# Last row and tail of a two-layer graph kernel: weight tiles in row slots, a written-out order, a two-pass last norm

## The reference

```python
def layer0(h, adj, W1, W2, b):          # h: 4096x128, adj: 4096x4096, K = 16
    node = h @ W1
    hw = einsum('nc,kcf->nkf', h, W2)
    x = einsum('nk,nkf->nf', node, hw)
    return relu(adj @ x + node @ b)
def layer1(z, dist, W, B):
    msg = z @ W + B
    weights = where(dist < 1, exp(-(1 / dist - 1) ** 2 / (2 * 0.5 ** 2)), 0)
    return weights @ msg
x = layernorm(x + layer0(x, adj, ...))
x = layernorm(x + layer1(x, adj, ...))
```

## Time and profile before

| | |
|---|---|
| median of three runs | 572.2 us |
| the profiled execution, its own time | 571.83 us |
| its span | 570.0 us |
| TensorE busy | 557.1 us (98%) |
| ScalarE busy | 506.7 us (89%) |
| VectorE busy | 478.5 us (84%) |
| granted TensorE clock, mean | 0.998 |
| DMA queue 1, share of 16 engines | 66.5% |

### The profile page before, as it was taken

The page is one execution under the profiler, slowest core; times in us unless marked ns, Lnnn a source line. Parts: engine busy times, 40 slices in busy tenths (PEclk is TensorE's granted clock), DMA queues, the critical chain, the costliest instruction groups (busy, mean ns, idle before and its releaser), DMA issues.

```text
span 570.0 us, 5196 instructions
## 1 busy us (share of the span) xinstructions
PE 557.1 (98%) x1794; PEld 328.4 (58%) x1794; DVE 478.5 (84%) x524; ACT 506.7 (89%) x458; POOL 82.8 (15%) x74
## 2 busy tenths in 40 slices
PE   9999999999999999999999999999999999979896
PEld 7888888555555645565556555655565556534344
DVE  6777777998959997998899979997998899779553
ACT  5788878799999999999998999899989998678984
POOL 2889999100000000000000000000000000000000
PEclk9999999999999999999999999999999999999999
DMA  5991000599988878888889878887888774462012
GB/s 170 411 419 44 20 1 0 197 385 424 385 314 322 298 293 295 314 317 305 302 301 341 303 287 315 308 326 282 324 325 324 280 298 148 147 221 75 0 55 92
DMA packets 23129, 142.04 MB, mean 249 GB/s; under 512 B 2720, under 2 KB 3264, under 8 KB 6720
## 3 DMA queue, kind: packets, MB, share of 16 engines
q1 hardware_dynamic: 22960, 141.46, 66.5%
q10 hardware_dynamic: 144, 0.26, 0.2%
HBM read 139.62 MB, written 2.10 MB: 249 GB/s over the span
## 4 chain that ended last, share of the span: by engine, by line
PE 68%; ACT 17%; DVE 9%; issue 4%; DMA 1%; SPq 0%; DVEq 0%; ACTq 0%
PE l_ps L452 20%; PE acc_ps L414 9%; PE kept_ps L452 6%; ACT wt_pair L573 5%; PE hw_ps L377 5%; PE hw_ps L383 5%; PE hw_ps L380 5%; ACT wt_pair L578 5%; DVE wt_pair L748 4%; PE acc_ps L405 4%; PE acc_ps L404 4%; PE acc_ps L403 4%; ACT wt_pair L583 3%; DVE wt_pair L742 3%; ACT wt_pair L593 2%
## 5 line engine op out<-in xcount | busy, mean ns | idle before, releaser
L452 PE MATMUL l_ps<-wt_pair,msg 128*128 128x512 f32 x376 | 168.9, 592 | 2.2 <-DVE sumT L793 2.2
L742 DVE SCALAR_TENSOR_TENSOR wt_pair<-wt_pair 128x2048 f32<-128x2048 f32 x64 | 146.0, 2284 | 7.4 <-DMA wt_pair<-adjT_dram 7.3
L573 ACT ACTIVATE wt_pair<-wt_pair 128x4096 f32<-128x4096 f32 (+1 forms) x37 | 116.5, 3147 | 3.4 <-DVE wt_pair L742 3.4
L452 PEld LDWEIGHTS l_ps<-wt_pair,msg 128*128 128x128 f32 x376 | 70.7, 190 | 84.4 <-issue 80.4
L578 ACT ACTIVATE wt_pair<-wt_pair 128x4096 f32<-128x4096 f32 (+1 forms) x37 | 116.9, 3159 | 1.2
L414 PE MATMUL acc_ps<-row_in,x 128*128 128x512 f32 x216 | 96.8, 592 | 0.0
L560 ACT ACTIVATE prods<-hw_ps,node 128x128 f32<-128x128 f32 x256 | 73.0, 373 | 17.3 <-PE hw_ps L383 15.7
L590 ACT ACTIVATE wt_pair<-wt_pair 128x4096 f32<-128x4096 f32 (+1 forms) x19 | 62.0, 3262 | 27.4 <-DVE wt_pair L748 27.4
L735 DVE TENSOR_TENSOR row_lo<-row_in,adj_hi 128x2048 fp32r<-128x2048 f32 x37 | 84.8, 2292 | 1.3
L748 DVE SCALAR_TENSOR_TENSOR wt_pair<-wt_pair 128x4096 f32<-128x4096 f32 (+1 forms) x19 | 75.4, 3969 | 9.7 <-ACT wt_pair L578 9.7
L702 DVE SCALAR_TENSOR_TENSOR part_acc<-hw_ps,node,part_acc 128x128 f32<-128x128 f32 x224 | 60.7, 344 | 19.2 <-PE hw_ps L383 19.2
(11 more groups left out here) (84 smaller groups left out, 491.9 us busy)
## 6 DMA issues: line engine op xcount, KB each, us to landing
row_in<-adjT_dram SPq DMA_DIRECT2D x64, 1024.0 KB, 4.8
wt_pair<-adjT_dram SPq DMA_DIRECT2D x64, 1024.0 KB, 4.8
x_in<-xT_dram SPq DMA_DIRECT2D x8, 256.0 KB, 4.0
x_row<-xT_dram SPq DMA_DIRECT2D x8, 256.0 KB, 5.1
outT_dram<-sumT SPq DMA_DIRECT2D x7, 256.0 KB, 2.0
W_in<-W_dram SPq DMA_DIRECT2D x3, 256.0 KB, 5.2
W_in<-W_dram ACTq DMA_DIRECT2D x1, 256.0 KB, 3.8
outT_dram<-sumT SPq DMA_DIRECT2D x2, 128.0 KB, 1.8
```

The source lines that it names most:

```text
L452: mm = pe.matmul(out, msg[:, c % 2, k, :], wt[t % WT_RING][:, k, :], start=(first and k == 0), stop=(last and k == CH - 1))
L573: act.activation(w, w, ACT.Ln, bias=TINY).then_inc(ln_made, 1)
L742: dve.scalar_tensor_tensor(out=w, in0=w, scalar=1.0, in1=w, op0=ALU.is_lt, op1=ALU.mult).then_inc(mask_made, 1)
```

## The change

Four things are changed:

1. Weight tiles 60 to 63 are loaded into the first four *row* slots (`IN_ROWS = 60`), as soon as row tiles 60 to 63, which lie there, are done; they have their own semaphores, and they are masked singly and go through ln and inverse in pairs like the others.
2. From step 56 on (`TAIL = 56`) the order on ScalarE and VectorE is written out: the whole last row and the tail. ScalarE's log and exp of a norm are separate steps now (`log_variance`, `inverse_root`), with other work between them.
3. From tile 54 on (`BY_TILE`) the square and the last exp are done by tile, 128 x 2048, where they were done by pair. From tile 50 on (`THIRD_FROM`) the shared banks are three, with `acc_ps[:, 0]` as the third. The banks of the last norm are dealt anew.
4. In units 3 to 6 of the last norm (`TWO_PASS`) centre and variance run on rounded operands: VectorE casts the operand and subtracts for the remainder (into `adj_hi`, which is free by then), and TensorE runs one matmul on each. The two matrices are rounded once, at step 32.

```diff
 SPLIT = (1, 3, 4, 5, 7)
 SPLIT_FIRST = ((3, 5, 7), (1, 3, 5, 7))
+SPLIT_LAST = (1, 3, 4, 5, 7)
 SPLIT_LEAD = 2
 
 
 FIRST_STEPS = (0, 3, 5, 7, 10, 12)
 FIRST_PAIR = len(FIRST_STEPS)
-DVE_FROM = 54
-LAST_PAIR = 60
-
-TAIL = 66
+
+BY_TILE = 54
+
+IN_ROWS = 60
+
+THIRD_FROM = 50
+
+TAIL = 56
+
+TWO_PASS = (3, 6)
 
 ...
 
 
     def in_pair(m):
-        return FIRST_PAIR <= m < LAST_PAIR
+        return m >= FIRST_PAIR
 
 
     groups = [m for m in range(TILES) if not in_pair(m) or m % 2 == 0]
     group_of = [len([m for m in groups if m <= t]) - 1 for t in range(TILES)]
 
     def is_split(i):
+        if i // NB == NB - 1:
+            return i % NB in SPLIT_LAST
         return i % NB in (SPLIT_FIRST[i // NB] if i < 2 * NB else SPLIT)
 
     def on_dve(m):
         if in_pair(m):
-            return (m - FIRST_PAIR) % 4 >= 2 or m >= DVE_FROM
-        return m >= LAST_PAIR
+            return (m - FIRST_PAIR) % 4 >= 2 or m >= BY_TILE
+        return False
 
     split_tiles = [i for i in range(TILES) if is_split(i)]
-    dve_groups = [m for m in groups if on_dve(m)]
+
+    parts = [m for m in groups if m < BY_TILE] + list(range(BY_TILE, TILES))
+    part_of = [len([m for m in parts if m <= t]) - 1 for t in range(TILES)]
+    dve_parts = [m for m in parts if on_dve(m)]
     act_groups = [m for m in groups if not on_dve(m)]
 
 ...
+    def in_two_pass(u):
+        return TWO_PASS[0] <= u <= TWO_PASS[1]
+
+
+    shared = [t for t in range(TILES) if t % NB >= KEPT]
+    bank_of, before = {}, {}
+    for n, t in enumerate(shared):
+        late = len([s for s in shared if THIRD_FROM <= s < t])
+        bank_of[t] = t % L1_BANKS if t < THIRD_FROM else (L1_BANKS + late) % (L1_BANKS + 1)
+        same = [s for s in shared[:n] if bank_of[s] == bank_of[t]]
+        before[t] = same[-1] if same else None
 
     def row_added_step(r):
         return NB * (r + 1) + (3 if r < NB - 1 else 2)
 ...
+            rows = sb("rows", [P, ROW_RING, CH, BW], F32, whole)
+            row_in = [rows[:, s, :, :] for s in range(ROW_RING)]
 ...
+        wt = [wt_pair[t % WT_RING // 2][:, t % 2, :, :] if t < IN_ROWS else row_in[t - IN_ROWS] for t in range(TILES)]
 ...
+        y2_hi = [adj_hi[0][:, s, :] for s in range(2)]
+        y2_lo = [adj_hi[0][:, 2 + s, :] for s in range(2)]
+        sq2_hi = [adj_hi[1][:, s, :] for s in range(2)]
+        sq2_lo = [adj_hi[1][:, 2 + s, :] for s in range(2)]
 ...
+        shared_ps = [l1_ps[:, 0, :], l1_ps[:, 1, :], acc_ps[:, 0, :]]
+        yc2_banks = [acc_ps[:, 1, :], yc_ps[:, :], kept_ps[:, 0, :]]
+        yc2_ps = [yc2_banks[u % 3][:, 0:width(u)] for u in range(UNITS)]
+
+        var2_ps = [var_ps[:, 0:width(u)] for u in range(UNITS - 1)] + [shared_ps[bank_of[LAST - 2]][:, 0:HALF_BW]]
+
+        last_ps = [shared_ps[bank_of[LAST]][:, 0:HALF_BW], kept_ps[:, 1, 0:HALF_BW]]
 ...
+            def load_last_wt(t):
+
+                sp.wait_ge(row_tile_done, t + 1)
+                sp.dma_start(wt[t], adjT[t % NB, t // NB]).then_inc(last_wt_in[t - IN_ROWS], 16)
 ...
+                if IN_ROWS <= i < TILES:
+                    load_last_wt(i)
                 t = i - COL_LAG
-                if t >= 0 and t + WT_RING < TILES:
+                if t >= 0 and t + WT_RING < IN_ROWS:
                     load_wt(t + WT_RING)
 ...
                 if j >= KEPT:
-
-                    at_least(pe, sum_added, added_to(t - L1_BANKS - (KEPT if j < KEPT + L1_BANKS else 0)))
-                    out, first, last = l1_ps[:, j % L1_BANKS, :], True, True
+                    if before[t] is not None:
+
+                        pe.wait_ge(sum_added, added_to(before[t]))
+                    elif t >= THIRD_FROM:
+
+                        pe.wait_ge(y_made, NB - 1)
+                    out, first, last = shared_ps[bank_of[t]], True, True
                 else:
                     out, first, last = kept_ps[:, j, :], c == 0, c == NB - 1
-                pe.wait_ge(wts_made, group_of[t] + 1)
 ...
-                pe.wait_ge(sum_added, added_to(LAST - L1_BANKS if half == 0 else TILES - NB))
-                pe.wait_ge(wts_made, group_of[LAST] + 1)
+                pe.wait_ge(sum_added, added_to(before[LAST] if half == 0 else TILES - NB + 1))
+                pe.wait_ge(wts_made, part_of[LAST] + 1)
 ...
             def centre2(u):
+                at_least(pe, out_made, u - 2)
+                if in_two_pass(u):
+                    pe.wait_ge(rounded_w_made, 2)
+                    pe.wait_ge(y2_lo_made, u - TWO_PASS[0] + 1)
+                    pe.matmul(yc2_ps[u], centre_r[:, :], y2_hi[u % 2], start=True, stop=False)
+                    pe.matmul(yc2_ps[u], centre_r[:, :], y2_lo[u % 2], start=False, stop=True).then_inc(yc2_made, 1)
+                    return
                 pe.wait_ge(sum_added, added_to(TILES - NB - 1) + u + 1)
-                if u < NB - 2:
-                    at_least(pe, out_made, u - 2)
-                if u == UNITS - 1:
-
-                    pe.wait_ge(out_made, 4)
                 pe.matmul(yc2_ps[u], centre_w[:, :], sumT[:, unit(u)], start=True, stop=True).then_inc(yc2_made, 1)
 
             def variance2(u):
+                if u < UNITS - 1:
+                    at_least(pe, ln_var2_made, u)
+                else:
+
+                    pe.wait_ge(sum_added, added_to(LAST - 2))
+                if in_two_pass(u):
+                    pe.wait_ge(sq2_lo_made, u - TWO_PASS[0] + 1)
+                    pe.matmul(var2_ps[u], mean_r[:, :], sq2_hi[u % 2], start=True, stop=False)
+                    pe.matmul(var2_ps[u], mean_r[:, :], sq2_lo[u % 2], start=False, stop=True).then_inc(var2_made, 1)
+                    return
                 pe.wait_ge(sq2_made, u + 1)
-                if u == UNITS - 2:
-
-                    pe.wait_ge(out_made, 5)
-                else:
-                    at_least(pe, ln_var2_made, min(u, NB - 1))
                 pe.matmul(var2_ps[u], mean_w[:, :], sq[:, u % 2, 0:width(u)], start=True,
                           stop=True).then_inc(var2_made, 1)
 ...
             def take_exp(m):
-                w = weights(m)
+                w = part(m)
                 if on_dve(m):
 
-                    act.wait_ge(dve_square_made, dve_groups.index(m) + 1)
+                    act.wait_ge(dve_square_made, dve_parts.index(m) + 1)
                     act.activation(w, w, ACT.Exp, bias=-2.0, scale=-2.0).then_inc(wts_made, 1)
                 else:
 ...
-                at_least(act, var2_made, u - 1)
+                if in_two_pass(u - 2):
+
+                    act.wait_ge(sq2_lo_made, u - 2 - TWO_PASS[0] + 1)
+                else:
+                    at_least(act, var2_made, u - 1)
                 act.activation(sq[:, u % 2, 0:width(u)], yc2_ps[u], ACT.Square).then_inc(sq2_made, 1)
+
+            def log_variance2(u):
+                act.wait_ge(var2_made, u + 1)
+                at_least(act, out_made, u - 1)
+                act.activation(rstd[:, u % 2, 0:width(u)], var2_ps[u], ACT.Ln, bias=EPS).then_inc(ln_var2_made, 1)
 
             def inverse_root2(u):
 ...
+            take_exp(46)
+            square(6)
 ...
+            take_exp(54)
+            take_inverse(56)
+            take_exp(55)
+            square(7)
+            take_ln(58)
+            log_variance(7)
+            take_exp(56)
+            inverse_root(7)
+            take_inverse(58)
 ...
+            def round_unit(u):
+                dve.wait_ge(sum_added, added_to(TILES - NB - 1) + u + 1)
+                if u < TWO_PASS[0] + 2:
+                    dve.wait_ge(row_tile_done, TILES)
+                else:
+                    dve.wait_ge(yc2_made, u - 1)
+                dve.tensor_copy(y2_hi[u % 2], sumT[:, unit(u)]).then_inc(y2_hi_made, 1)
+
+            def remainder_of_unit(u):
+                dve.wait_ge(y2_hi_made, u - TWO_PASS[0] + 1)
+                dve.tensor_tensor(y2_lo[u % 2], sumT[:, unit(u)], y2_hi[u % 2], ALU.subtract).then_inc(y2_lo_made, 1)
+
+            def round_square2(u):
+                dve.wait_ge(sq2_made, u + 1)
+                if u < TWO_PASS[0] + 2:
+                    dve.wait_ge(row_tile_done, TILES)
+                else:
+                    dve.wait_ge(var2_made, u - 1)
+                dve.tensor_copy(sq2_hi[u % 2], sq[:, u % 2, :]).then_inc(sq2_hi_made, 1)
+
+            def remainder_of_square2(u):
+                dve.wait_ge(sq2_hi_made, u - TWO_PASS[0] + 1)
+                dve.tensor_tensor(sq2_lo[u % 2], sq[:, u % 2, :], sq2_hi[u % 2], ALU.subtract).then_inc(sq2_lo_made, 1)
 ...
+                if i == TILES // 2:
+                    dve.wait_ge(mean_w_filled, 1)
+                    dve.tensor_copy(mean_r[:, :], mean_w[:, :]).then_inc(rounded_w_made, 1)
+                    dve.wait_ge(centre_w_filled, 2)
+                    dve.tensor_copy(centre_r[:, :], centre_w[:, :]).then_inc(rounded_w_made, 1)
 ...
+            residual(7)
+            mask(60)
+            mask(59)
+            add_part(50)
 ...
+            round_unit(5)
```

(3 more changed lines are left out.)

216 lines of the change are left out of this document (144 added, 72 removed).

## The result

| | before | changed |
|---|---|---|
| median | 572.0 us (571.64 to 574.16, 4 runs) | 563.59 us (562.16 to 565.01, 4 runs) |
| profiled execution, its own time | 571.83 us | 562.98 us |
| its span | 570.0 us | 561.2 us |

The ratio is 0.9837 with an interval of 0.9805 to 0.9868: 1.6% faster. The forecast was 562.9 us. The two profiled executions are 8.85 us apart, against 9.35 in the sum.

A forecast was written before the change was run, and what follows sets the result against it. TensorE bounds up to row tile 63, waits between engines matter only behind it. Savings of 5.75 + 3.2 + 0.4 = 9.35 us off 571.8 give 562.5, with 0.4 us offset a median of 562.9 us; range 561.5 to 567.0.

The forecast's parts named there:

- What bounds the kernel: TensorE is the bound up to the end of row tile 63; waits between engines cost only in the last 76 us.
- The walk: ScalarE and VectorE queues followed through the new order with measured durations, setting ready against needed times, TensorE dense from 493.97 us.
- The three holes: TensorE's waits ahead of variance(7), column tile 53 and centre2(0) close: 1.2 + 2.5 + 2.05 = 5.75 us.
- The two passes: Units 3 to 6 of the last norm: eight matmuls on rounded operands save 0.402 us each, 3.2 us.
- Rival 1: Units 3 to 6: rounding on VectorE becomes the pace and the 3.2 us are lost, 566.1 us; chance 0.14.
- near misses: Remainders of units 3 and 5 on VectorE, ready just before TensorE wants them: cover 0.6 and 0.25 us, costed at nothing.
- The closing chain: From the start of centre2(8) to the end of the last finish: 3.7 instead of 4.1 us, saving 0.4 us.
- The row slots: Weight tiles 60 to 63 load earlier, into row slots; by itself this costs TensorE nothing.
- Work by tile: Splitting late squares by tile costs 0.05 us each on VectorE and lets the first exp start 2.2 us sooner.
- Rival 2: The three holes reappear elsewhere with their size, only 3.2 us are gained, 569.0 us; chance 0.09.
- rival 3: Weight tile 59's load lands late, delaying mask(59), the messages' copy and column tile 56: 575 us; chance 0.05.

The follow-up runs named there:

- e1: The changed kernel with units 3 to 6 of the last norm back in float32, without rounding; median 565.66 us, ratio 0.9871 to the kernel before.
- e4: The changed kernel with the ScalarE and VectorE order of the kernel before, up to tile 61; median 572.28 us, ratio 0.9969 to the kernel before.
- e9: The changed kernel with the old order up to tile 61 and units 3 to 6 in float32; median 572.39 us, ratio 1.0004 to the kernel before.
- e8: The changed kernel with three spare casts on VectorE ahead of the scale of row 7; median 567.88 us, ratio 0.9908 to the kernel before.
- e7: The changed kernel with four spare casts on VectorE ahead of the scale of row 7; median 568.27 us, ratio 0.9935 to the kernel before.
- e3: The changed kernel with weight tiles 60 to 63 back in column slots, masks 59 and 60 swapped; median 569.85 us, ratio 0.9939 to the kernel before.
- e5: The changed kernel with squares and last exps of tiles 54 to 63 by pair again; median 569.94 us, ratio 0.9949 to the kernel before.

## Why the prediction was right, step by step

**What bounds the kernel.** The prediction said "up to the end of row tile 63 TensorE is the bound, and only behind it do waits between engines cost anything": TensorE is busy 54.00 of 54.00 us in the first window in both kernels, and the gain is found behind it.

**The walk.** With 0.62 us added, it gives 501.2, 504.0 and 509.6 for the adds of tiles 50, 51 and 52, 517.4 for the copy, and 524.2 and 527.0 for the adds of 56 and 57. These are the times at which each is ready. The rows end at 501.34, 504.13, 509.74, 517.54, 524.34 and 527.14: all six 0.1 us later than the walk, which counted 0.60 us for an operation whose row lasts 0.68. Column tile 56 was due at 518.6 and started at 518.65; centre2(0) 525.5 and 525.52. The three holes were to close for 5.75 us, and 5.67 came.

**The two passes.** 8 x 0.402 = 3.2 us forecast, 3.19 by stage and 3.14 when taken out. Of the two rules weighed there, the rows decided both. By the figure of the Trainium skill ("TensorE: Matmul & The Clock Gate", Back-to-back issue gap) the estimate would have been 4.8 us; the two rounded matmuls of a unit still follow each other after 0.22 to 0.24 us (545.34, 545.56, then 545.80). By the rule of the Trainium skill ("VectorE: DVE Perf Modes", The DRAIN you can't avoid) as the prediction took it, the estimate for the second remainder of unit 5 was near 552.4; the same section adds that an operation that is not held back starts earlier, and the rows go by that (0.60 us into one of 0.68). The remainder ends at 551.46 + 0.69 = 552.15, and its matmul starts at 552.35, where a dense TensorE was due at 552.3. Rival 1, rounding as the pace, did not occur, though its near misses were as near as feared: unit 3's remainder ends at 538.91 + 0.68 = 539.59, in front of a due time of 540.1.

**The closing chain.** 0.4 us forecast, 0.58 came: the term was sized a little too small. From the start of centre2(8) to the end of the last finish it is 559.01 - 555.50 = 3.5 us, not 3.7. With the 0.62 us added the walk has it from 555.36 to 559.07 us: its end came true, and centre2(8) started 0.14 us later than it said. No run takes this part out by itself. e1, e4 and e9, which keep the new order there, have 3.14, 3.09 and 3.15 us from the start of centre2(8) to that of the last finish, against 3.67 before.

**The row slots.** "By itself this costs TensorE nothing" is right, but the text gave no price for being without them. With the tiles back in the column slots the stretch is 6.7 us longer: mask(60) waits for its load. They are a condition of the order.

**Work by tile.** Here a sentence was wrong. The split was priced at "0.05 us each on an engine with slack", with a first exp that starts 2.2 us sooner, and left at that. The price is right (two squares of a tile in a row take 508.43 - 504.02 = 4.41 us in e4_old_order) and the use was missed: without it 6.4 us come back, since it is the split that lets an add stand between two squares.

**Rivals 2 and 3.** No hole moved elsewhere, and tile 59's load (rival 3) delayed nobody: mask(59) starts at 498.45 without a wait. How a hole would have been priced was too low, though. Rival 2 counted holes by their length, and in six of the experiments a hole of 2.1 to 4.2 us cost 1.7 to 2.9 us more than that through the clock. Had it come true, it would probably have been slower than 569.0: in e4_old_order, where three holes of 5.92 us together are back, the stretch is only 1.49 us shorter than before, and not 3.2.

So the gain of 9.4 us is not a sum of four changes. Slots, bank and tiles alone (with the order of the closing chain) give a ratio of 1.0004; with the two passes 0.9969; the new order makes it 0.982 to 0.984, and it needs the slots and the tiles. Taken out of the whole, the third bank changes nothing.

## What to carry to other kernels

When one engine is nearly dense, write down for each thing it waits for when it will be ready and when it is wanted, walking the queues of the helping engines with measured durations; here six such times and the end came out within 0.15 us. Small operations that release the busy engine (the adds) belong between the long ones, and long ones should be split where one must be passed, even if the split itself saves nothing. Price a hole in TensorE as its length plus the slow matmuls that may follow, and test parts of such a change by taking one out of the whole, since each alone can look worthless.

## What the runs showed of the hardware

**A short hole can halve TensorE's clock for some microseconds.** In the profiled executions:

| run | hole, us | clock behind it | slower by, us |
|---|---|---|---|
| before, ahead of column tile 53 | 2.39 | 1.00 | 0.1 |
| before, ahead of centre2(0) | 1.97 | 1.00 | 0.1 |
| e4 and e9, ahead of the messages | 1.79 | 1.00 | 0.1 |
| e8 | 2.10 | 0.57, then 1.00 | 1.77 |
| e4 | 2.68 | 0.72, 0.68, then 1.00 | 1.80 |
| e9 | 2.68 | 0.58, then 0.99 | 1.8 |
| e7 | 3.43 | 0.50, 0.79, then 1.00 | 1.73 |
| e3 | 3.77 | 0.50, 0.81, then 1.00 | 2.88 |
| e5 | 4.15 | 0.59, 0.78, then 1.00 | 1.81 |

The window of the kernel before behind its hole of 2.39 us:

```profile
510.40:514.00 3.60, 3.56 (x9) 1.65 (x10) 3.60 (x4) 3.57 (x4) 0.00 (x0) 1.00 0.56 232
```

In these executions the loss hardly depends on the length of the hole: 1.7 to 1.8 us in five of six. Of the holes in the table those over 2.5 us brought the clock down, those under 2 us did not, and between them one did (2.10) and one did not (2.39). Length alone therefore does not decide. It also differs between executions of one program, as far as their mean clocks tell. Of e8's four executions three had 0.996 to 0.997 and took 567.87 to 568.23 us, and one had 1.000 and took 565.84. With longer holes one execution of e4 (569.62 us), two of e7 and three of e9 had 0.999 or 1.000. Of e3's six, four had 0.994, like the profiled one that lost 2.88 us, and two 0.996. The kernel before had 0.998 when profiled, with a fall only at its very end, where TensorE has no more work, but 0.995 or 0.996 in 12 of its 52 executions beside the experiments: its holes may not always have been harmless. What a fall costs is read from the profiled executions alone: the times of the others also carry the shift of the next paragraph, which is as large, and e7's two at 0.999 were no faster than those at 0.996. The Trainium skill ("TensorE: Matmul & The Clock Gate", Part 1: The HAM clock gate) says that half clock is the default that only activity lifts, and that the chip's judging is not in step with the kernel, so that the same kernel comes out differently from run to run. The two levels and e8's four executions agree with that; the rule of thumb there for how long a gap is harmless does not hold here, where 2.10 us did harm. What sets apart the holes of 2.10 and 2.39 us was not tried further and stays open.

**Executions of one program differ by 2 us ahead of the last stretch.** The changed kernel took 561.98, 562.20, 562.29 and 564.65 us in one series, all at a mean clock of 1.00. The profiled one, the longest, has its bias matmul of row 7 at 496.21 us, where the first profile has 494.59, and the same 64.0 us from there to the last finish. What makes the difference ahead of it was not looked into. For a change at the end of a program a stretch between two marks in the trace is the sharper measure: it repeated within 0.04 us.
